# Adapter product, layer norm and int8 FFN on one core: FFN weight rows dealt out by eights, two loop periods written out, one sum moved to GpSimd, and new orders on every engine

## The reference, cut to what matters

```python
# x: (8, 256, 1024) f32; ids: (8,) in 1..14; weight: (16, 1024, 1024) f32
y = einsum('bij,bkj->bik', x, weight[ids])           # one adapter matrix for each batch
h = (y - mean) * rsqrt(var + 1e-5) * gamma + beta    # over the last dimension
h = quant(h) @ quant(w1).T + b1                      # quant: per row, scale = max|.|/127, rounded
h = gelu(h)
h = quant(h) @ quant(w3).T + b3
out = x + h
```

## Time and profile before

| | |
|---|---|
| median of 3 runs | 357.23 us (355.5 to 359.37) |
| the profiled execution's own time | 357.55 us |
| its span | 355.7 us |
| TensorE busy | 333.7 us (94%) |
| GpSimd busy | 264.2 us (74%) |
| VectorE busy | 284.5 us (80%) |
| ScalarE busy | 220.4 us (62%) |
| mean granted TensorE clock | 0.981 |

### The profile page before, as it was taken

The page is one execution under the profiler, slowest core; times in us unless marked ns, Lnnn a source line. Parts: engine busy times, 40 slices in busy tenths (PEclk is TensorE's granted clock), DMA queues, the critical chain, the costliest instruction groups (busy, mean ns, idle before and its releaser), DMA issues.

```text
span 355.7 us, 5548 instructions
## 1 busy us (share of the span) xinstructions
PE 333.7 (94%) x1744; PEld 230.7 (65%) x1744; DVE 284.5 (80%) x346; ACT 220.4 (62%) x230; POOL 264.2 (74%) x160
## 2 busy tenths in 40 slices
PE   6899996999988999999999999999999999996994
PEld 6788885856755666665766576566666666763442
DVE  0488765949769888797888888888979888999596
ACT  2335486645988457775688379737975588524670
POOL 1505629406898988997999799988998899937552
PEclk9899999899999999999999999999999999999898
DMA  7999999794865989929991999479955945150006
GB/s 252 351 377 374 349 156 248 165 241 158 231 121 100 239 251 222 192 68 297 210 217 42 293 227 213 84 217 281 207 121 152 299 103 155 62 177 1 2 0 236
DMA packets 48714, 68.39 MB, mean 192 GB/s; under 512 B 5046, under 2 KB 40118, under 8 KB 48698
## 3 DMA queue, kind: packets, MB, share of 16 engines
q1 hardware_dynamic: 48698, 68.19, 74.6%
HBM read 59.79 MB, written 8.40 MB: 192 GB/s over the span
## 4 chain that ended last, share of the span: by engine, by line
PE 57%; DVE 13%; DMA 11%; POOL 8%; issue 5%; ACT 4%; SPq 2%; DVEq 0%; ACTq 0%; POOLq 0%
PE f_ps L1283 17%; PE a_ps L1205 11%; PE a_ps L1207 10%; PE a_ps L1206 10%; DMA w_nat<-in_L_cond_weight 6%; DMA x_res<-in_L_ffn_w 4%; POOL a L538 2%; DVE x_nat L1019 2%; PE t_ps L1335 2%; PE f_ps L1260 2%; DVE t_ps L898 1%; DVE h_max L939 1%; POOL y L520 1%; POOL x_lo L543 1%; POOL y L518 1%
## 5 line engine op out<-in xcount | busy, mean ns | idle before, releaser
L1205 PE MATMUL a_ps<-w_hi,x_hi 128*128 128x512 f32 x248 | 103.9, 419 | 0.5 <-ACT y L672 0.2
L1207 PE MATMUL a_ps<-w_hi,x_lo 128*128 128x512 f32 x248 | 97.0, 391 | 0.0
L1206 PE MATMUL a_ps<-w_lo,x_hi 128*128 128x512 f32 x248 | 96.6, 390 | 0.0
L1283 PE MATMUL f_ps<-w_q,q_t 128*128 128x512 bf16 x400 | 90.7, 380 | 3.1 <-ACT q_t L707 2.2
L1283 PEld LDWEIGHTS f_ps<-w_q,q_t 128*128 128x128 bf16 x400 | 37.1, 98 | 51.0 <-issue 5.5
L898 DVE STREAM_TRANSPOSE t_ps<-w_nat 128x1024 f32<-128x1024 f32 x48 | 59.3, 1244 | 9.6 <-DMA w_nat<-in_L_cond_weight 8.5
L657 ACT ACTIVATE w_hi<-t_ps 128x1024 fp32r<-128x1024 f32 x48 | 48.3, 1019 | 23.8 <-DVE t_ps L898 23.5
L904 DVE TENSOR_TENSOR w_lo<-t_ps,w_hi 128x1024 fp32r<-128x1024 f32 x48 | 57.3, 1215 | 3.3 <-ACT w_hi L657 3.3
L1205 PEld LDWEIGHTS a_ps<-w_hi,x_hi 128*128 128x128 f32 x248 | 46.6, 188 | 12.0 <-ACT y L672 1.0
L1207 PEld LDWEIGHTS a_ps<-w_hi,x_lo 128*128 128x128 f32 x248 | 46.5, 188 | 10.4
L538 POOL TENSOR_TENSOR a<-a,rows 128x1024 f32<-128x1024 f32 x14 | 34.5, 2461 | 25.2 <-DVE a L971 23.4
(11 more groups left out here) (156 smaller groups left out, 497.8 us busy)
## 6 DMA issues: line engine op xcount, KB each, us to landing
w_nat<-in_L_cond_weight SPq DMA_DIRECT2D x96, 256.0 KB, 5.7
x_res<-in_x SPq DMA_DIRECT2D x7, 1024.0 KB, 7.3
out<-o SPq DMA_DIRECT2D x14, 512.0 KB, 3.1
x_nat<-in_x SPq DMA_DIRECT2D x24, 256.0 KB, 10.2
w_nat<-in_L_cond_weight SPq DMA_DIRECT2D x10, 512.0 KB, 5.8
w_q<-in_L_ffn_w SPq DMA_DIRECT2D x4, 512.0 KB, 6.8
h_r<-in_L_cond_weight SPq DMA_DIRECT2D x4, 512.0 KB, 5.6
w_scale_row<-in_L_ffn_w SPq DMA_DIRECT2D x3, 512.0 KB, 10.2
```

Of the source, the lines that this page charges most:

```text
L1205: pe.matmul(ps, hi, w_hi[:, u, c], start=begin, stop=False)
L1206: pe.matmul(ps, hi, w_lo[:, u, c], start=False, stop=False)
L1207: last = pe.matmul(ps, lo, w_hi[:, u, c], start=False, stop=end)
L1283: last = pe.matmul(ps[:, half, :], q[:, c, :], w[:, c, half_of(half)], start=c == 0, stop=c == CB - 1)
```

## The change: what it does

Five things.

1. **Rows to tiles.** Tile i of `w1` (and of `w3`) held rows 128i to 128i+127. Now partition p of tile i holds row 8p+i. So the eight scales of a partition belong to eight neighbouring rows, and `store_scales` writes 128 pieces of 32 B in place of 1024 pieces of 4 B. `take_prep` puts the tile's columns back in order: it writes its bf16 results 8 elements (16 B) apart in `w_q`, where it wrote 128 neighbouring ones.
2. **Loop.** The periods p = 2 and p = 6 are written out on all engines; the loop runs over 3, 4 and 5.
3. **x plus b3 of the last batch** (`residual_last`, two instructions of 128x1024) moves from VectorE to GpSimd.
4. **New orders** in the prologue, in the period and at the end, on all five queues.
5. The wait for the ids moves into the loads that use them.

```diff
@@ SyncE @@
             def load_first_unit(u, parts=range(2)):
+                sp.wait_ge(ids_loaded, 16)
...
-                    src = (w1, w3)[i // RT][(i % RT) * P:(i % RT + 1) * P, :]
+                    src = (w1, w3)[i // RT].rearrange("(p i) d -> i p d", i=RT)[i % RT]
...
-                sp.dma_start(scale_scratch[n].rearrange("(i p) -> p i", p=P), wq_scale[:, RT * n:RT * (n + 1)],
-                             allow_slow_non_contiguous=True
+                sp.dma_start(scale_scratch[n].rearrange("(p i) -> p i", p=P), wq_scale[:, RT * n:RT * (n + 1)]
                              ).then_inc(scales_stored[n], 16)
...
             load_first_x((0,))
-            sp.wait_ge(ids_loaded, 16)
-            load_first_x((1,))
             load_prep((2,))
             load_first_unit(0)
+            load_first_x((1,))
             load_rows()
...
-            load_rows_of_w((7,))
-            store_scales(0)
-            load_prep((9,))
             load_prep((12,))
             load_prep((10,))
+            load_rows_of_w((7,))
+            load_x(2)
+            store_scales(0)
             load_unit(2, 1)
-            load_x(2)
...
@@ GpSimd, period @@
                 add_b1(p - 1, 0)
                 low_x(p + 1, 0)
-                add_b1(p - 1, 1)
-                residual(p - 1)
                 normalisers_of(p)
                 low_x(p + 1, 1)
+                add_b1(p - 1, 1)
                 scale_and_shift(p, 0)
                 scale_and_shift(p, 1)
+                residual(p - 1)
                 finish(p - 1, 0)
                 finish(p - 1, 1)
...
+            def residual_last(t):
+                pool.wait_ge(x_last_loaded, 16)
+                pool.tensor_tensor(x_last[:, t], x_last[:, t], b3_row, ALU.add).then_inc(x_last_ready, 1)
...
@@ ScalarE, take_prep @@
-                    rows_of_tile = slice((i % RT) * P, (i % RT + 1) * P)
-                    act.activation(w_q[i // RT][:, :, rows_of_tile], whole_words(f_ps[:, i % 2], I16), ACT.Copy
+                    act.activation(w_q[i // RT][:].rearrange("p c (k i) -> p c i k", i=RT)[:, :, i % RT],
+                                   whole_words(f_ps[:, i % 2], I16), ACT.Copy
                                    ).then_inc(wq_ready, 1)
...
@@ TensorE, period @@
+                piece(p, 2, 0)
                 transpose_h(p - 1, 0)
                 transpose_h(p - 1, 1)
-                piece(p, 2, 0)
+                piece(p, 2, 1)
                 ffn1(p - 1, 0)
-                piece(p, 2, 1)
-                ffn1(p - 1, 1)
                 piece(p, 3, 0)
                 piece(p, 3, 1)
+                ffn1(p - 1, 1)
+                piece(p + 1, 0, 0)
                 transpose_g(p - 1, 0)
-                piece(p + 1, 0, 0)
+                piece(p + 1, 0, 1)
                 ffn2(p - 1, 0)
-                piece(p + 1, 0, 1)
+                piece(p + 1, 1, 0)
                 transpose_g(p - 1, 1)
-                piece(p + 1, 1, 0)
+                piece(p + 1, 1, 1)
                 ffn2(p - 1, 1)
-                piece(p + 1, 1, 1)
...
@@ TensorE, prologue @@
             transpose_first(2)
+            piece(0, 0, 0)
             transpose_first(3)
-            piece(0, 0, 0)
...
@@ VectorE, end @@
-                residual_last(0)
-                residual_last(1)
```

More of the change, by code:

```diff
@@ L458, in _ @@
[L458 to L466, removed]
-            store(0, 1)
-            with sp.Fori(2, LAST - 1) as p:
-                period(p)
-            period(LAST - 1)
-            load_residual(LAST - 1)
             def store_last(t, half):
@@ new lines, in _ @@
+            load_prep((13,))
+            load_x(3)
+            load_unit(2, 2)
+            load_unit(2, 3)
+            store_scales(1)
+            load_residual(0)
+            load_scale_row(1)
+            load_unit(3, 0)
+            load_x(4)
+            load_unit(3, 1)
+            load_unit(3, 2)
+            load_unit(3, 3)
+            store(0, 0)
+            store(0, 1)
+            load_residual(1)
+            load_unit(4, 0)
+            load_unit(4, 1)
+            store(1, 0)
@@ L484, in _ @@
+            store(1, 1)
+            with sp.Fori(3, LAST - 1) as p:
+                period(p)
+            load_unit(LAST, 2)
+            load_residual(LAST - 2)
+            load_unit(LAST, 3)
+            load_last_x()
+            store(LAST - 2, 0)
+            store(LAST - 2, 1)
+            load_residual(LAST - 1)
             store(LAST - 1, 0)
+            store(LAST - 1, 1)
             store_last(0, 0)
-            store(LAST - 1, 1)
             store_last(0, 1)
@@ L607, in _ @@
             finish(0, 1)
-            with pool.Fori(2, LAST) as p:
+            add_b1(1, 0)
+            low_x(3, 0)
+            low_x(3, 1)
+            normalisers_of(2)
+            add_b1(1, 1)
+            scale_and_shift(2, 0)
+            scale_and_shift(2, 1)
+            residual(1)
+            finish(1, 0)
+            finish(1, 1)
+            with pool.Fori(3, LAST - 1) as p:
                 period(p)
@@ L874, in _ @@
             round_h(1, 1)
+            copy_y(2, 0)
             scale_ffn2(0, 1)
             split_w(2, 3, 1)
[L877 to L879 removed]
+            split_w(3, 0, 0)
+            take_h(1)
+            split_w(3, 0, 1)
+            split_x(3, 0)
+            split_w(3, 1, 0)
+            gelu(1, 0)
+            split_x(3, 1)
+            copy_y(2, 1)
+            round_g(1, 0)
+            split_w(3, 1, 1)
+            normalise(2, 0)
+            take_g(1, 0)
+            gelu(1, 1)
+            split_w(3, 2, 0)
+            split_w(3, 2, 1)
+            normalise(2, 1)
+            round_g(1, 1)
+            scale_ffn2(1, 0)
+            split_w(3, 3, 0)
+            take_g(1, 1)
+            split_w(3, 3, 1)
+            round_h(2, 0)
+            round_h(2, 1)
+            copy_y(3, 0)
+            scale_ffn2(1, 1)
+            with act.Fori(3, LAST - 1) as p:
                 period(p)
@@ L1435, in ffn2_last_quarter @@
                     last.then_inc(ffn2_done, 1)
-                transpose_h(f, 0)
-                transpose_h(f, 1)
+                piece(LAST - 1, 2, 0)
+                transpose_h(LAST - 2, 0)
+                transpose_h(LAST - 2, 1)
+                piece(LAST - 1, 2, 1)
+                piece(LAST - 1, 3, 0)
+                ffn1(LAST - 2, 0)
+                piece(LAST - 1, 3, 1)
+                ffn1(LAST - 2, 1)
+                piece(LAST, 0, 0)
+                transpose_g(LAST - 2, 0)
+                piece(LAST, 0, 1)
+                ffn2(LAST - 2, 0)
+                piece(LAST, 1, 0)
+                transpose_g(LAST - 2, 1)
+                piece(LAST, 1, 1)
+                ffn2(LAST - 2, 1)
                 unit(2, 0)
@@ L1528, in _ @@
             transpose_g(0, 1)
+            piece(2, 1, 1)
             ffn2(0, 1)
-            piece(2, 1, 1)
-            with pe.Fori(2, LAST) as p:
+            piece(2, 2, 0)
+            transpose_h(1, 0)
+            transpose_h(1, 1)
+            piece(2, 2, 1)
+            ffn1(1, 0)
+            piece(2, 3, 0)
+            piece(2, 3, 1)
+            ffn1(1, 1)
+            piece(3, 0, 0)
+            transpose_g(1, 0)
+            piece(3, 0, 1)
+            ffn2(1, 0)
+            piece(3, 1, 0)
+            transpose_g(1, 1)
+            piece(3, 1, 1)
+            ffn2(1, 1)
+            with pe.Fori(3, LAST - 1) as p:
                 period(p)
```

362 lines of the change are left out of this document (223 added, 139 removed).

## The result

| | before | changed |
|---|---|---|
| median | 357.81 us (4 runs, 355.5 to 359.37) | 403.44 us (4 runs, 400.8 to 403.87) |
| ratio | | 1.127 [1.118, 1.135], slower |
| span of the profiled execution | 355.7 us | 402.0 us |
| mean granted TensorE clock | 0.981 | 0.936 |

The forecast was 346.5 us, and its range ended at 353. The changed kernel takes 403.

What follows compares the result with a forecast made beforehand. TensorE, busy 94% of the span, was taken as the bound. Terms -2.3 - 5.7 - 0.1 - 4.1 + 4.0 - 1.7 - 1.0 = -10.9 from 357.55 gave 346.65, so about 346.5 us; range 342 to 353.

Steps and rivals of the forecast that it cites:

- Seven tiles in a row: Prologue's end: seven consecutive tile transposes wait for VectorE, then for ScalarE emptying two banks; a new cost of +4.0 us.
- rival C: take_prep's spread write is slow: 356.5 us at 1.9 a tile, 368.5 at 3.1; chances 0.06 no change, 0.05 slower.
- The rule against the change: take_prep's writes: skill says accesses each in another 16-byte line pay a penalty, size not given; speaks for slower writes.
- Start: Kernel start: first weights land 1.5 us sooner, products skip a 0.9 us transpose wait, clock may hold; -2.3 us.
- Store: Prologue: 128 store pieces for 1024, placed behind three tiles, remove the 4.32 us stall and slow clock; -5.7 us.
- FFN products: Batches 0 and 1: 2.8 us pieces cover waits before FFN products, and period 2's transpose waits go; together -4.1 us.
- -0.1: Prologue: the 0.70 us wait at 48.99 goes, but tile 6 waits about 0.6 for ScalarE; together -0.1 us.
- Rival A: Prologue: full queue, not the store, made the tile late; 4 of the 5.7 stay, 350.5 us; chance 0.13.
- The period: Periods 3 to 6: a piece ahead of the transposes and an ffn2 covering y's copy save -1.7 us.
- the 1.0 of period 2: Period 2: transposes' waits of 0.36 and 0.65 us are covered by an extra piece; counted within the -4.1.
- Rival B: Loop becomes bound by the chain through GpSimd, 1 us a period over five; 351.5 us, chance 0.12.
- The end: After the last period: sums moved off VectorE, statistics 1.5 us sooner, GpSimd collision possible; -1.0 us (-2.1 to +1.3).

Runs made afterwards that it cites:

- e5: Separate kernel, only copying 1024 elements a partition at several steps on ScalarE, then VectorE; ScalarE's bf16 write took 1.02 us side by side, 4.69 at 16 B steps.
- e1: Changed kernel with take_prep writing side by side, columns left permuted (does not compute the reference); 350.23 us, ratio 0.979 against before.
- e4: Kernel before with dealt rows and the 32 B store, old orders, writes side by side (does not compute the reference); 349.82 us, ratio 0.977.
- f1: Changed kernel with old rows, writes side by side, 32 B store kept, VectorE putting the scale row in order; 349.6 us, ratio 0.975 against before.
- e2: Changed kernel's new orders with old rows, writes side by side and the 4 B scale store; 354.11 us, ratio 0.986 against before.
- f3: f1 with x plus b3 of the last batch later on GpSimd, behind residual and add_b1; 347.63 us, ratio 0.971 against before.
- f2: f1 with x plus b3 of the last batch back on VectorE, ahead of the last statistics; 347.74 us, ratio 0.970 against before.

## Why the prediction was wrong, point by point

**The failing step** is one price in "Seven tiles in a row" and in rival C: `take_prep` at 1.03 us. It is 4.96 us by the record and 4.55 to 4.6 in a row (32.10 us for seven). The prediction said that no row has such a write, took the nearest row, and set 3.1 us as the upper end without a row for it. Its argument against C was that ScalarE takes 1.0 us for 1024 elements whatever type it writes, "so the writing has slack". That row is about width. e5 shows it says nothing of the step: f32 side by side still takes 1.02 us, and bf16 at 16 B steps 4.69. So C was the right mechanism with a wrong bound and too small a chance. It went the way that C had described: the seven in a row pay in full, 32.1 us on the chain, and the nine earlier ones, which "pass an engine busy two thirds of that time", pay too. Even C's slope was too flat. Its 22 us for 2.07 us a tile (3.1 for 1.03) are 10.6 us for each microsecond, 42 us for 3.93; measured are 54.2 in the prologue (162.31 for e1's 108.12), 86% of the 63 us that the sixteen records grew by. When the seven start, the changed kernel is 27.7 us behind e1 (111.47 for 83.79), which is 78% of 9 x 3.93 us, and from there to W2 it loses another 26.5. So the nine earlier ones were not half hidden, as C had it: ScalarE, busy 44.50 of 46.00 us there, has next to no idle time left to hide them in. By C's own slope, too, "slower by 1%" begins at about 2.4 us a tile and not at 2.2.

**The rule against the change.** The row of the changed kernel shows 4.96 us for 1.03. The Trainium skill (SBUF — State Buffer, section "Door 1: The DMA port swizzle") says that an access in another 16-byte line pays; a penalty there is, and the sign of the forecast hung on it, but its size does not go by lines (f32 and bf16 at 16 B steps, 1.96 and 4.69 us). Its statement that one may stride 8 bf16 or 4 fp32 for free is not what e5 measured: 1.30, 2.43 and 4.69 us at 2, 4 and 8 bf16, and 1.96 at 4 fp32, for 1.02. The measurement decides.

**Start, forecast -2.3.** The first weights were transposed at 9.21 us, 0.45 sooner and not 1.5. SyncE issued their load only 0.74 us sooner (3.06 for 3.80); why the landing gained still less is open. But the clock held:

```profile
9.21 1.09 PE L1468 MATMUL t_ps<-ident,w_nat 128*128 128x128 f32 x8 [1.13 <-DMA w_nat<-in_L_cond_weight]
10.71 1.09 PE L1468 MATMUL f_ps<-ident,w_nat 128*128 128x128 f32 x8 [0.41 <-DMA w_nat<-in_L_cond_weight]
```

The second takes 1.09 us for the 1.86 of the earlier trace rows. Why it held with almost the same waits in front was not settled. At the third piece of weights, with the same work behind it, the changed kernel is 1.88 us ahead (15.52 for 17.40). So the term came near its -2.3, with less from the load and more from the clock than reckoned: its size is in part luck.

**Store, FFN products, seven in a row: -5.7, -0.1, -4.1, +4.0.** Near once the write is put aside, though the sum hides that the store was put too low. e1's prologue is 8.5 us shorter; the parts that belong to it sum to 7.2 with the start. The wait ahead of the seven was 0.93 (forecast 1.1), their pace 0.92 us (forecast 1.0). e4 shows that 6.2 us of the prologue come with the 32 B store and no new order, and 8.0 of the whole span (355.7 to 347.7), for the 5.7 of the forecast. Rival A (the store is not the cause) is out by e4, which alters nothing in the order of the queue, and by f1, which has the old rows. That the store's stall cost only by way of the load behind it, as the chain of the earlier trace rows had it, fits e4 and e2; it was not tried by itself.

**The period, -1.7 and the 1.0 of period 2.** Five periods are 184.73 us, 3.3 less; the forecast was 2.7. But e4, with the old orders, has 186.27: its TensorE has none of the waits of the earlier trace rows in period 2. So 1.75 of the 3.3 come with the store, and the new orders are worth 1.5. TensorE has no gap there. Rival B (GpSimd binds) is out: GpSimd is busy 137.29 of 150.24 and TensorE never waits for it.

**The end, forecast -1.0.** It is +3.9 in e1 and in the changed kernel, outside the term's bounds of -2.1 and +1.3. The prediction named the collision and gave it +1.3 by the rule (the Trainium skill, SBUF — State Buffer, section "Who interferes with whom": an operation of VectorE with two inputs in SBUF contends with GpSimd's reads). The trace agrees with the rule, 3.39 us for 1.28. The size was too small: the two sums were taken to fill time in which VectorE's path does not need GpSimd, while three of its four gamma and beta steps meet GpSimd's stream (the first of them, 3.35 us at 302.14, meets `finish`, which the new order put between the normalisers, and it stays in f3), and TensorE waits for the last and comes out slow. By the table, the sum's place is worth 2.3 us of the end (f1 to f3), 2.9 with the sum on VectorE (f2, whose end is 345.5 less 294.72, 50.78). The other 1.25 of the 3.9 lie between e1 and f1, which have the same orders at the end: it is the slow stretch at 329.47 in e1. Why the clock fell there is open: f2 waited 2.34 us at this place and kept its clock.

With the end at +3.9 in place of -1.0, the same sum gives 357.55 - 9.9 + 3.9 = 351.6 us for the change without its write, where e1 took 350.2; the write is the other 53. That the sum misses e1 by only 1.4 us is in part luck: the store alone was put 2.3 us too low.

## What to carry to other kernels

When a change makes an engine write (or read) elements apart, the row of the same operation side by side is no price for it: measure that one form by itself, or take as the upper end the time for all the bytes that it steps over (8 x 1.02 us here, which holds the 4.69; no run shows that it always would). Put an order right on the smallest operand, here one row of 1024 scales for each of the two matrices in place of 2 million weights. And before moving an operation to a less busy engine, look at what its neighbour has to do at that moment: each moved sum was 2.34 us of work on GpSimd, and with them there two steps of VectorE took 3.4 us longer, one beside a sum and one beside the `add_b1` that follows it.

## What the hardware showed that I had not expected

- Writing 1024 bf16 elements a partition at steps of 2, 4, 8 and 16 B: 1.02, 1.30, 2.43, 4.69 us on ScalarE; VectorE 0.69 side by side and 4.68 at 16 B. f32 at steps of 4, 8, 16 and 32 B: 1.02, 1.07, 1.96, 2.00. At 16 B steps a bf16 element costs 2.4 times an f32 element.
- Reading f32 at 32 B steps costs ScalarE 2.03 us for 1.06, VectorE 1.08 for 0.69.
- 4 KB in 4 B pieces took 10.7 us to land in before and 14.1 in e2; in 32 B pieces 4.1 in the changed kernel, 5.4 in e4 and 8.3 in e1. With the 32 B pieces in the old order (e4) TensorE's 4.32 us stall was gone, which had stood behind a load of 512 KB.
- VectorE's beta step, 1.28 us by itself, took 3.35 at 302.14 in e1, beside a GpSimd operation of 2.40 that had started at 302.01: it ended 1.08 us after that operation.
